# A decoder layer over eight batches: where ScalarE copies each attention group's sums out of PSUM

## What is computed

```python
x = _layernorm(x + linear_memory(x))            # k, v, q = x W + b; state <- 0.99 state + 0.01 v k^T; y = (state q) Wo + bo
x = _layernorm(x + cross_attention(x, ctx))     # 16 heads of 16 columns
x = _layernorm(x + self_attention(x) + moe(x))  # 16 heads of 16 columns; 8 experts, the best 2 by a softmax gate

scores = einsum('bhqd,bhkd->bhqk', qh, kh) / sqrt(16)
attn = softmax(scores, axis=-1)
out = einsum('bhqk,bhkd->bhqd', attn, vh)
```

## Time and profile before

| | us |
|---|---|
| median of three runs | 1263.95 |
| the runs | 1262.15 to 1264.09 |
| the profiled execution | 1261.23 |
| its span, first to last instruction | 1259.4 |
| TensorE recorded busy | 1207.8 |
| VectorE | 918.7 |
| ScalarE | 778.6 |
| GpSimd | 381.9 |

### The profile page before, as it was taken

How to read it: one execution, slowest core, us unless ns; L and a number is a source line. 1 busy time by engine, 2 the same in 40 slices (tenths; PEclk the granted TensorE clock), 3 DMA queues, 4 the chain that set the end, 5 groups by cost and what they waited for, 6 DMA issues and landing times.

```text
span 1259.4 us, 20675 instructions
## 1 busy us (share of the span) xinstructions
PE 1207.8 (96%) x7004; PEld 601.2 (48%) x7004; DVE 918.7 (73%) x1867; ACT 778.6 (62%) x1090; POOL 381.9 (30%) x485
## 2 busy tenths in 40 slices
PE   8789999999999999999999999999999999999998
PEld 4443444545445445444454454454454544544443
DVE  3587786678777787777877777777777778678772
ACT  2255556665576665766657665667557666665664
POOL 5510103411622134420523206231153204430261
PEclk9899999999999999999999999999999999999999
DMA  7422122112222122222122222122122211212200
GB/s 249 117 56 65 43 52 66 46 46 56 62 67 58 39 68 56 56 69 51 46 66 66 57 58 65 44 72 52 39 56 69 52 36 43 68 28 52 52 18 18
DMA packets 56446, 74.99 MB, mean 60 GB/s; under 512 B 14720, under 2 KB 26520, under 8 KB 56088
## 3 DMA queue, kind: packets, MB, share of 16 engines
q1 hardware_dynamic: 55192, 72.96, 23.2%
q10 hardware_dynamic: 1152, 0.72, 0.2%
HBM read 18.06 MB, written 4.19 MB: 18 GB/s over the span
## 4 chain that ended last, share of the span: by engine, by line
PE 80%; DVE 7%; ACT 6%; issue 4%; SPq 2%; DMA 1%; POOL 0%; ACTq 0%; DVEq 0%
PE ms L480 36%; PE op L480 16%; PE sc L480 15%; PE mx L480 9%; DVE maxes L984 3%; PE ms L590 2%; ACT probs L798 2%; SPq L427 2%; PE ms L531 2%; ACT moe L791 1%; PE ms L585 1%; DVE q_parts L894 1%; ACT k_parts L734 1%; ACT q_parts L734 0%; ACT oT L733 0%
## 5 line engine op out<-in xcount | busy, mean ns | idle before, releaser
L984 DVE TENSOR_REDUCE maxes<-mx 128x1 f32<-128x512 f32 x1024 | 657.7, 684 | 209.4 <-PE mx L480 207.6
L798 ACT ACTIVATE probs<-sc 128x1024 f32<-128x1024 f32 x512 | 525.1, 1026 | 365.2 <-PE sc L480 361.2
L1234 POOL TENSOR_TENSOR x<-x,moe 128x256 f32<-128x256 f32 x256 | 187.5, 732 | 653.8 <-ACT moe L791 632.2
L480 PE MATMUL op<-probs,v 128*32 128x512 f32 x2048 | 272.8, 604 | 7.1 <-ACT oT L733 6.8
L480 PE MATMUL sc<-qs,ks 50*128 50x512 f32 x1024 | 256.3, 497 | 12.0 <-ACT probs L798 11.1
L480 PEld LDWEIGHTS sc<-qs,ks 50*128 50x128 f32 x1024 | 95.3, 183 | 304.7 <-ACT probs L798 232.4
L480 PE MATMUL mx<-ks,qs 48*128 48x512 f32 x1024 | 209.7, 404 | 13.5 <-DVE maxes L984 12.5
L791 ACT ACTIVATE moe<-ms,comb 128x256 f32<-128x256 f32 x256 | 107.0, 473 | 24.0 <-PE ms L480 24.0
L480 PEld LDWEIGHTS mx<-ks,qs 48*128 48x128 f32 x1024 | 97.4, 187 | 25.5 <-DVE maxes L984 20.5
L480 PE MATMUL ms<-we_hi,x2T_hi 128*128 128x512 f32 x256 | 92.8, 443 | 3.2 <-DVE q_parts L894 1.0
L480 PEld LDWEIGHTS op<-probs,v 128*32 128x32 f32 x2048 | 40.7, 108 | 100.9 <-issue 99.3
(11 more groups left out here) (155 smaller groups left out, 1303.9 us busy)
## 6 DMA issues: line engine op xcount, KB each, us to landing
ks<-k_parts SPq DMA_DIRECT2D x384, 64.0 KB, 2.3
qs<-q_parts SPq DMA_DIRECT2D x381, 64.0 KB, 2.2
xT_s<-in_xT SPq DMA_DIRECT2D x8, 512.0 KB, 3.9
x_s<-in_x SPq DMA_DIRECT2D x8, 512.0 KB, 4.3
out<-x SPq DMA_DIRECT2D x7, 512.0 KB, 3.2
x_s<-in_ctxT SPq DMA_DIRECT2D x6, 512.0 KB, 5.1
qs<-shift_r SPq DMA_DIRECT2D x128, 8.0 KB
x<-in_ctxT SPq DMA_DIRECT2D x2, 512.0 KB, 6.4
```

Of the source, the lines that this page charges most:

```text
L480: return nc.tensor.matmul(dst, lhsT, rhs, start=first, stop=last, skip_group_check=True)
L798: nc.scalar.activation(probs[:, (2 * s + h) % 3, :, :], sc[:], ACT.Exp).then_inc(exp_out, 1)
L984: nc.vector.tensor_reduce(maxes[:, g % 2, at:at + 1], mx[:, i % 3, :], AX_X, ALU.max).then_inc(max_out, 1)
L1234: nc.gpsimd.tensor_tensor(x2[:, n % 2, t, :], x2[:, n % 2, t, :], moe[:, k % 2, j * D:j * D + D], ALU.add).then_inc(acc, 1)
```

## The change

In the loop over half-slots on ScalarE, the copy of every group's sums is now issued ahead of the exp of its half-slot, and no longer only for the three groups of `wanted`. No instruction is added or removed, and the waits of each stay as they are. `wanted` goes on to decide where the `heads` units are planned.

```diff
                 for task, k, n in OTHERS["act"][t]:
-                    if task == "oT" and wanted(k):
+                    if task == "oT":
                         other(task, k, n)
                 if 0 <= s < SLOTS * len(PHASES):
                     exps(s, h)
...
                 for task, k, n in OTHERS["act"][t]:
-                    if not (task == "oT" and wanted(k)):
+                    if task != "oT":
                         other(task, k, n)
```

## The result

| | before | after |
|---|---|---|
| median of twelve runs each, same chip (us) | 1263.74 | 1259.54 |
| the runs | 1261.03 to 1267.74 | 1256.11 to 1262.59 |
| the profiled execution | 1261.23 | 1261.07 |
| its span | 1259.4 | 1259.3 |

The ratio is 0.9969, with a 95% interval of 0.9956 to 0.9983. The two profiled executions, however, are equal.

What follows compares the result with a forecast made beforehand. TensorE was taken as the bound, so ScalarE's order matters only where TensorE waits. Gains of 5.49 us less losses of 1.04 made -4.45 us, which from the median 1263.95 gave 1259.5 us, range 1256.8 to 1263.5.

Steps and rivals of the forecast that it cites:

- The reading of the bound: TensorE, busy 96%, sets the time; its 6.8 us of value-matmul waits in ten places about cap the gain; VectorE follows.
- The price and the cover: Early copies delay ScalarE's exps, 16.6 us over 61 places; TensorE's remaining units hide this in 57 half-slots.
- The thin places: Groups 53 and 58 to 61: least spare TensorE time after the exp, 0.64 us against a 0.45 delay in group 59.
- The losses: Scores of groups 7, 62 and 51 wait longer for delayed exps: 0.48, 0.48 and 0.08, sum 1.04 us.
- The gains: Value matmuls stop waiting for the copy in ten groups, 4, 6, 9, 17, 25, 33, 41, 49, 50, 56: 5.49 us.
- The six: Groups 9, 17, 25, 33, 41, 49: next slot's exp starts 0.48 earlier; TensorE regains 0.66 us each, 3.96 together.
- Rival 1: Something unseen holds the next slot's exp at 710.65 in group 33; net -1.2 us, 1262.8, no measurable change; chance 0.15.
- rival 2: Next scores follow the value matmuls, not the exp; seven places give 0.92 each, net -6.3 us, 1257.6; chance 0.10.
- Rival 3: Delayed exps reach TensorE's scores after moved copies: up to 16.6 us, net +11, 1275, slower; chance 0.05.

Runs made afterwards that it cites:

- the ten alone: Kernel before, copy issued early only in the ten groups whose value matmuls waited for it, plus the three that had it: 1256.56 us, ratio 0.9955.
- all others: Kernel before, copy issued early in the other 51 groups and left late in the ten whose value matmuls waited: 1263.23 us, ratio 1.0003.
- three copies: Changed kernel with each of the 61 moved copies issued three times ahead of the exp, output unchanged: 1281.21 us, ratio 1.0131 to before.
- the held take-outs: Kernel before, no copy moved; in groups 9, 17, 25, 33, 41, 49 two `moe` take-outs issued after first-half exps: 1256.60 us, ratio 0.9943.

## Why the prediction was right

**The reading of the bound held.** Time came from the ten waits of the value matmuls and from nowhere else: the ten alone give 0.9955, all others 1.0003. VectorE followed, its waits for TensorE's `mx` fell from 207.6 to 203.2 us.

**The price and the cover.** The delays on ScalarE came out as tabulated: none in eight places, 0.09 in ten, about 0.30 in 26 and 0.42 to 0.47 in 17. But for groups 7, 62, 50 and 51 each is taken back by the next exp. The thin places, groups 53 and 58 to 61, showed no loss in after, and with three copies they lost as a cover of 0.64 lets them.

**The losses.** Groups 7 and 62: 0.47 and 0.48 in the exps, 0.49 in the waits, for 0.48. Group 51: its exp is 0.09 late, for 0.08, but the loss doesn't last. Two slots on, TensorE's max matmuls wait 0.17 for VectorE where they wait 0.25 in the run that spares this group, and it is gone; the prediction counted it in full. The kernel without these three has the ratio 0.9958 against 0.9969, which is 1.4 us, but the intervals overlap; its trace is 1.7 us better, of which 1.0 is groups 7 and 62 and some 0.6 an earlier context DMA.

**The gains.** Groups 4 and 56 gave 0.37 each for 0.39, group 6 gave 0.66 for 0.66, group 50 0.08 to 0.12 for 0.09. The six gave 0.64 to 0.66 each. The distance between the `op` of groups 9 and 49, 744.2 before, is 741.1 after, where 740.9 was foretold:

```profile
263.34 1.06 PE L480 MATMUL op<-probs,v 128*32 128x512 f32 x8
...
1004.48 1.06 PE L480 MATMUL op<-probs,v 128*32 128x512 f32 x8
```

The exp of the next slot starts 0.83 after its scores, to the hundredth as forecast. What ended last behind the removed wait had been named, the `moe` take-out, and the run that held it back confirmed it.

**Sum.** -4.3 us in the trace against -4.45, -4.2 in the medians.

**Rivals.** Rival 1 (something unseen holds the next exp) and rival 2 (the whole wait comes back) fall with the same row, the exp at 708.91, 0.83 behind its scores: not held at 1.31, and late enough to take 0.25 of the gain. Rival 3 is a real mechanism that needs a larger price: with three copies it makes the kernel 1.3% slower, with one it costs lasting time in groups 7 and 62 alone.

**What was luck.** That the median, 1259.54, came out on the forecast 1259.5 is luck: the interval of the ratio is 1.7 us to either side, and the forecast started from a median of three runs. The prediction also put no price on stretches at half clock, and the profiled execution of after lost 3.0 us in one. Had after been judged by its span alone, a correct forecast would have looked like no change.

**A version that beats both.** The early copy but for groups 7, 51 and 62, with the held take-outs: 1253.63 us, 0.72% below before. The early copy everywhere gives 0.3% alone and the held take-outs 0.6%, and they overlap, since they remove the same wait in six groups.

## What to carry to other kernels

When a matmul waits for a copy in another engine's queue, look at what stands directly ahead of the copy: here it was a take-out of 0.8 us, and moving either of the two was enough. Price a move in an in-order queue by the delay of the next instruction and by the time the consumer still has work, place by place; 51 of 61 moves here bought nothing, and two of them cost. Then name what is late next before the wait is credited in full: of 0.92 us, 0.66 came back.

## What the runs showed of the hardware

- **Half-clock stretches come and go between profiled executions, and one can cost 3.0 us where the effect is 4.2.** The waits of 0.40 and 0.92 us ahead of the same matmuls were followed by a stretch at 1.2 GHz in four of the eight kernels' profiled executions: of the changed kernel, of the 51 others and of the held take-outs alone, 3.0 us each time, and of the three copies, 1.6 us. (In that of the held take-outs alone it begins 0.2 us before the second wait ends.) They were followed by none in those of before, of the ten places, of the three spared and of the best version. In that of the 51 others one more, 2.3 us, follows waits of 0.88 and 0.30 at 77 and 78 us that every one of the eight has. Of the three longest waits of the three copies, 1.76, 1.95 and 1.76, the first two were followed by one and the third was not; nor was a wait of 1.14 to 1.16 us near 270 in any of the eight. The runs' times go with their mean granted clock: of the kernel before, 1260.5 to 1261.9 at 0.996 and 1264.7 to 1267.9 at 0.989; of after, 1256.1 and 1258.4 at 0.996 and 1261.9 at 0.989. At the same 0.993 after has 1259.7 to 1261.1 and before, beside the first four experiments, 1263.2 to 1264.7, so the gain is not a difference in clock. What decides whether the clock falls behind a wait stays open.
- **Recorded idle time of a matmul can be less than what its cause costs.** Rows with 0.17 and 0.18 us of idle gave back 0.24 and 0.25; the idle time is counted from the modelled end of the matmul before, which is the likely reason. The distance from start to start (1.25 against 1.00) told the size.
- **One load moves the time by half a microsecond from one profiled execution to the next.** ScalarE waited 0.44 us for a context load in the profile of before and 0.54 in that of after; in those of the 51 others, of the three spared, of the best version and of the three copies this half microsecond is gone at the same slot. Each is one execution of another kernel, so what moves the load stays open. The row of before:

```profile
675.11 1.15 ACT L733 ACTIVATE ctxT_hi<-x_s 128x512 fp32r<-128x512 f32 x2 [0.44 <-DMA x_s<-in_ctxT]
```
